# Attention: TensorE turns the probabilities of a unit one slot later

## What is computed

```python
xq, xk = _apply_rope(xq), _apply_rope(xk)        # 32 query heads of 16, 8 key heads
scores = einsum('bhsd,bhtd->bhst', xq, keys) * scale
scores = where(causal, scores, -inf)
probs = softmax(scores, axis=-1)
out = einsum('bhst,bhtd->bhsd', probs, values)
return out @ w_o
```

## Time and profile before

| what | us |
|---|---|
| median of 3 runs (1770.57 to 1771.24) | 1770.59 |
| the profiled execution, its own time | 1775.06 |
| its span, first to last instruction | 1773.3 |
| PE busy | 1657.3 |
| DVE busy | 1081.9 |
| ACT busy | 796.5 |
| POOL busy | 607.9 |

### The profile page before, as it was taken

One profiled execution on the slowest core, in us unless ns is written; L12 is line 12 of the kernel. 1 busy time (PEld: TensorE's weight loads), 2 busy tenths in 40 slices (PEclk: granted clock), 3 DMA queues, 4 the chain that ended last, 5 costly groups with the idle time before them and its releaser, 6 DMA issues. The chain is left out here.

```text
span 1773.3 us, 26150 instructions
## 1 busy us (share of the span) xinstructions
PE 1657.3 (93%) x8965; PEld 1384.0 (78%) x8965; DVE 1081.9 (61%) x2298; ACT 796.5 (45%) x1723; POOL 607.9 (34%) x792
## 2 busy tenths in 40 slices
PE   5999999999999999999999999988999999999884
PEld 4898987888888888777877887867877878778773
DVE  7888876525566554674243324557776877777772
ACT  4676764222233222222122222137777777776860
POOL 5465553211111112341111112374354344444422
PEclk9999999999999999999999999989999999999996
DMA  3100001000111101321011012200000000000000
GB/s 123 34 25 13 14 30 46 25 24 22 30 35 33 35 23 46 110 75 51 22 31 40 28 36 65 60 24 13 1 13 1 13 7 7 13 1 13 13 7 19
DMA packets 32967, 54.26 MB, mean 31 GB/s; under 512 B 3840, under 2 KB 9120, under 8 KB 32832
## 3 DMA queue, kind: packets, MB, share of 16 engines
q1 hardware_dynamic: 32832, 52.55, 9.8%
HBM read 43.10 MB, written 9.44 MB: 30 GB/s over the span
## 5 line engine op out<-in xcount | busy, mean ns | idle before, releaser
L1266 POOL TENSOR_TENSOR m_a_lo<-m_prod,m_a_hi 128x512 fp32r<-128x512 f32 x100 | 134.5, 1345 | 638.4 <-ACT m_a_hi L1348 638.4
L1342 ACT ACTIVATE m_prod<-a_ps 128x512 f32<-128x512 f32 x100 | 59.9, 599 | 544.9 <-PE a_ps L128 544.8
L1501 DVE TENSOR_TENSOR m_prod<-m_prod,a_ps 128x512 f32<-128x512 f32 x100 | 68.8, 688 | 386.1 <-ACT m_prod L1342 386.1
L2058 ACT ACTIVATE t_p<-a_ps,t_nmax 128x128 f32<-128x128 f32 (+1 forms) x512 | 181.8, 429 | 96.5 <-DVE t_nmax L2155 96.3
L2155 DVE TENSOR_REDUCE t_nmax<-a_ps 128x2 f32<-128x512 f32 (+1 forms) x192 | 131.6, 685 | 50.2 <-PE a_ps L2238 27.6
L2161 DVE TENSOR_TENSOR t_pT_lo<-a_ps,t_pT_hi 128x512 fp32r<-128x512 f32 x192 | 131.3, 684 | 44.5 <-ACT t_pT_hi L2051 44.1
L2244 PE MATMUL a_ps<-consts,t_p 128*128 128x128 f32 x768 | 119.9, 279 | 23.1 <-ACT t_p L2058 21.7
L2244 PEld LDWEIGHTS a_ps<-consts,t_p 128*128 128x128 f32 x768 | 87.4, 141 | 47.2 <-ACT t_p L2058 41.5
L128 PE MATMUL a_ps<-m_hT_hi,m_w_lo 128*128 128x512 f32 x312 | 124.0, 397 | 0.0
L126 PE MATMUL a_ps<-m_hT_hi,m_w_hi 128*128 128x512 f32 x312 | 123.1, 395 | 0.4 <-DVE f_w_lo L1406 0.4
L127 PE MATMUL a_ps<-m_hT_lo,m_w_hi 128*128 128x512 f32 x312 | 123.3, 395 | 0.0
(11 more groups left out here) (287 smaller groups left out, 4688.8 us busy)
## 6 DMA issues: line engine op xcount, KB each, us to landing
m_raw<-in_w_mlp SPq DMA_DIRECT2D x75, 256.0 KB, 2.7
a_xt<-in_x SPq DMA_DIRECT2D x8, 512.0 KB, 3.8
t_yl<-in_x SPq DMA_DIRECT2D x16, 256.0 KB, 4.5
x_store<-stream SPq DMA_DIRECT2D x4, 1024.0 KB, 5.2
t_yl<-x_store SPq DMA_DIRECT2D x16, 256.0 KB, 2.7
out<-t_yl SPq DMA_DIRECT2D x16, 256.0 KB, 2.0
m_raw<-in_w_attn SPq DMA_DIRECT2D x10, 256.0 KB, 2.8
a_att<-in_w_mixer SPq DMA_DIRECT2D x8, 256.0 KB, 2.8
```

Of the source, the lines that this page charges most:

```text
L1266: pool.tensor_tensor(a_lo[:, n % 2, :], prod[:, :], f(a_hi[:, n % 2, :]), ALU.subtract).then_inc(lo, 1)
L1501: dve.tensor_tensor(prod[:, :], prod[:, :], ps[:, U + TURN_AT["unit", n, 0] % 2, :], ALU.mult).then_inc(prodd, 1)
L2058: last = act.activation(p[:, u % 2, h * width:(h + 1) * width], unit_bank(u)[:, h * width:(h + 1) * width], ACT.Exp, bias=nmax[:, u % 3, h ...
```

## The change

In the loop over the slots PE turns the probabilities of unit s - 1 where it turned those of unit s. All else stays: the other engines' lists, the buffers, the waits of each operation.

```diff
         for s in range(first, end):
             if 0 <= s + 1 < SLOTS:
                 scores(s + 1)
             if 0 <= s - PT_RING < SLOTS:
                 values(s - PT_RING)
-            if 0 <= s < SLOTS:
-                transposes(s)
+            if 0 <= s - 1 < SLOTS:
+                transposes(s - 1)
             for what, part, t, b in JOBS[s]:
```

## The result

| what | before | after |
|---|---|---|
| median of 5 runs each, us | 1771.24 (1770.57 to 1775.13) | 1779.62 (1778.9 to 1785.18) |
| the profiled execution, its own time | 1775.06 | 1779.27 |
| its span | 1773.3 | 1777.5 |
| first scores of unit 0, from the span's start | 1186.81 | 1182.73 |
| from there to the end of the span | 586.49 | 594.77 |

The kernel became **slower by 0.53%**: ratio 1.0053, 95% interval 1.0038 to 1.0068. The two profiled executions differ by only 4.2 us. The last two rows say why: attention happened to begin 4.1 us earlier in the one of after, in work that the change doesn't touch. So I read every kernel from the first scores of unit 0 on. There the change costs 8.3 us, which fits the medians' 8.4. That they agree to 0.1 is luck: behind the last scores the profiles of before, late_14_18 and wait_3_4_8, whose orders are alike there, take 54.7, 56.2 and 54.4 us.

What follows compares the result with a forecast made beforehand. PE was taken as nearly full, its largest wait 21.7 us for exponentials. Terms 3.0 + 1.8 + 1.8 + 1.0 - 2.4 gave 5.2 us longer, 1775.8 us; range 1763 to 1784 (8 in 10).

Steps and rivals of the forecast that it cites:

- n = 15 to 18 and n = 1: Slots where PE's transposes waited for exponentials: PE would only arrive earlier at the same next release; gain 0.
- A: From n = 22 on: `low` starts 0.65 us late, delaying DVE's work through to x; 3.0 us over 5 batch passages.
- B: n = 5 and 6: late `high` delays exponentials and the drain of x on ACT; 0.3 us in 6 batches, 1.8 us.
- C: n = 9 and 10: late `high` delays ACT's copy of v, then hT_lo; 0.3 us in 6 batches, 1.8 us.
- D: The end: last transposes move behind the values of slot 192, so ACT copies the output block later; 1.0 us longer.
- E: Batches 0 and 7, with few side jobs on PE: a gain of 2.4 us, between bounds 0 and 8.3.
- Rival 1: The terms cancel: time 1770.6, give or take 3.5; chance 0.28.
- Rival 2: Faster, PE keeping its lead through n = 15 to 18 as drains come earlier; 1748.9, likelier 1763.4; chance 0.17.
- Rival 3: Slower: PE's scores wait for `low` and the delay goes round with every unit; 15 us, 1785.6; chance 0.05.
- Rival 4: The change does nothing: each wait reappears as long in the same slot; counted within rival 1.
- signs of being right: L2244's wait under 4 us, kT's grown by about that loss, hT_lo's about 8 us, batches of 70.3 to 71.5 us.
- sign of being wrong: Batches shorter than 69.5 us with kT waits as before, or L2231 and L2236 waiting for DVE's t_pT_lo.

Runs made afterwards that it cites:

- late_14_18: Kernel before with only the units of n = 14 to 18 (40 of 192) turned a slot late; ratio 0.9995 to the kernel before.
- wait_3_4_8: Kernel before, PE's order kept, with ACT's `high` also waiting for the next unit's transposes at n = 3, 4 and 8 only; ratio 1.0037.
- wait_21_23: Kernel before, PE's order kept, with ACT's `high` also waiting for the next unit's transposes at n = 21 to 23 only; ratio 1.003.
- before_low_last: Kernel before with `low` moved to the end of DVE's list of a slot, behind the layer-norm work; ratio 0.9934 to the kernel before.
- wait_all: Kernel before, PE's order kept, with ACT's `high` also waiting for the next unit's transposes, for every unit; ratio 1.0128.

## Why the prediction was right, and what in it was off

The direction, the mechanism and the range held: 1779.62 in a range of 1763 to 1784. The rise of the median was 8.4 us against the kernel before in the same comparison, where I summed 5.2. The profile's 8.3 can be laid out by term. The 0.56 that the profile of before had too much at the seam is added back, which makes 8.8.

| term | predicted | measured | where from |
|---|---|---|---|
| n = 15 to 18 and n = 1 | 0 | 0 | late_14_18, -0.02 a batch |
| A | 3.0 (5 x 0.6) | 4.0 | 0.71 in 5 passages, 0.42 in one more, into batch 1 |
| B | 1.8 (6 x 0.3) | 1.4 | 0.37 in batch 1, 0.21 in 5 batches |
| C | 1.8 (6 x 0.3) | 1.6 | 0.26 to 0.28 in 6 batches |
| D | 1.0 | 0.6 | last scores to the end |
| E, batches 0 and 7 | -2.4 | +1.0 | 0 in batch 0, +1.03 in batch 7 |
| the rest of batches 1 to 6 | 0 | 0.2 | |

- **What the change removes: right.** L2244 has no wait left in batches 1 to 6, and the gain is zero, as argued from the ends of the waits behind it. My upper bound of 21.7 us was no bound, since PE's busy time seems to have held part of the wait. In batches 2 to 6 wait_21_23 and wait_3_4_8 show the other half: the cost is the wait on ACT and nothing else of the new order.
- **A: right in place and chain, a little small.** I read 0.65 from the rows and took 0.6, for a stall of 0.2 at n = 3 that would be won on the way. It wasn't won; the step is 0.71. And the delay into batch 1 counts too, as it eats a lead of PE.
- **B and C: right in place.** C's 0.27 is the growth of one bracket. B came in two pieces, 0.12 and 0.18, less 0.09 won at units 3 to 6.
- **D: right to 0.1 at its head.** The last weighed output is turned 11.59 us after the last scores, before 10.66: 0.93. From there to the end the thirteen profiles take 41.5 to 45.6 us, so the 0.6 of the whole term is only what this one shows.
- **The sum of A to D** is 7.6 both as predicted and as measured. That is luck in part: A was 1.0 too small, B, C and D together 1.0 too large.
- **E: the mis-sized term, 3.4 us of 3.6 missed.** I took a direct gain of 2.4 because PE has few side jobs there and waits 8.3 us. The lead was real, 2.2 us at n = 5 beyond the 0.57 of the other kernels, but the added wait took it: 0.6 us by way of rope, and 1.5 when the granted clock fell behind the longer stand. In batch 7 hT_lo cost 1.0 at C's place. I had traced the next wait in every slot of the inner batches and not in these two, and had no term for the clock.
- **Rival 1** (terms cancel) fell: A to C are 7.0, more than the 6.6 that I took. **Rival 2** (faster) fell with late_14_18. **Rival 3** exists in traces: PE's scores wait 3.6 us for `low` in the whole kernel, 2.6 of it in batch 7, and the delay doesn't go round. **Rival 4** fell, since ACT's and DVE's waits are new in kind and cost time.
- The signs of being right came: kT's wait up by 8.6 us, hT_lo's from 4.3 to 7.0 (I had said about 8), batches of 70.9 to 71.5 us from unit 0 to unit 0 in batches 2 to 6, where those of before take 69.7 to 70.1. One sign of being wrong came as well, L2231 and L2236 waiting for DVE's t_pT_lo, the 3.6 us of rival 3; it was too small to decide anything.

The wait kernels give the price of a late input at the head of an in-order list: 0.71 us a batch at one place of ACT's, 0.56 at three others, at a granted clock of 1.00. The Trainium skill has the order (PSUM — Partial Sum Buffer, Engine vs sequencer instructions: strict FIFO), and these runs agree.

All of L2244's wait went and the time rose, while before_low_last had as much of it as before and took 0.66% off. The Trainium skill's advice is to find the gaps on the contended engine and to make what ends them start sooner or finish faster (Perfetto Trace Analysis, Optimization Strategy). The change didn't do that: it moved the instruction that waits, and the exponentials came no sooner. before_low_last did it for the gap ahead of the turn of h, where `low` stood in the way of xf, and there the advice is borne out.

## What to carry to other kernels

A wait on the busiest engine is worth only what lies between its end and the end of the next wait in the same slot; follow the freed engine to that next release, in the first and last rounds as well as in the steady ones. When producer and consumer are moved one slot apart, list what stands behind the consumer in its own in-order queue: it all inherits the delay. And where an instruction waits in a helper engine's list, first try to put ready work ahead of it; here that gave 12 us where the reordering of the busiest engine lost 8.

A stand of the matmul engine can cost more than its own length, since the granted clock may fall behind it: here 0.6 us more of standing was followed by 1.5 us lost at 0.50. Read the granted clock of every stretch in which a lead appears or goes.

To test such a reordering, add the wait alone to the kernel before: it shows the cost at its place, with no seam where one slot has the work twice. Take care that the wait isn't tighter than that of the change, as it was in wait_all.

## What I had not expected

- The start of attention scatters from 1180.6 to 1188.5 us between the profiles of kernels that are alike up to there, more than the whole effect. Counted from the first scores, term A's step has the same mean, 0.71, in all five kernels that hold it.
- The wait alone costs 22.6 us, 2.7 times as much as the wait with the later turn. For a delayed `high`, PE's order of the change is the better one; the delay is what costs.
